# Last V spread from two queues, first group normed and turned directly behind the modulation, new instruction orders

## The chip, the core and the metric
The kernel runs on one core of a Trainium2 chip. The core has five engines with a queue of instructions each: PE (matrix products; PEld is its weight load), DVE, ACT and POOL (elementwise work) and SP, which here only issues DMAs. An engine works its queue strictly in order, and engines wait for each other through semaphores. The metric is the device time of one execution in microseconds, the median of several runs.

## The reference, cut to what matters
Two layers follow each other, all in float32, on x of 32 sequences with 32 tokens of 128 features.

```python
# layer 0: a block with adaptive normalisation, 16 heads of 8 channels
shift, scale, gate, shift2, scale2, gate2 = split(silu(c) @ w_ada + b_ada, 6)
x_mod = ln(x) * (1 + scale) + shift
k, q, v = split(x_mod @ w_qkv, 3)
y = softmax(q @ k.T / 8) @ v                      # per head, 32 keys
x = x + gate * (y @ w_proj + b_proj)
x = x + gate2 * (gelu((ln(x) * (1 + scale2) + shift2) @ w_mlp1 + b_mlp1) @ w_mlp2 + b_mlp2)
# layer 1: graph attention in two directions d over the first 20 tokens
self_feat = concat(x, c or 0) @ W_self.T + b_self
out = self_feat + sum_d(softmax(q_d @ k_d.T / sqrt(8) + mask_d + label_d) @ kv, then Wout_d, + bout_d)
x = x + relu(out)
```

## The kernel before
128 partitions hold four sequences of 32 tokens; eight such groups g = 0 to 7 make the whole input. Layer 0 works up to the attention in five chunks (groups 0; 1; 2-3; 4-5; 6-7), the rest in four pairs of groups. An attention unit is one group (layer 0, units 0 to 7) or one group and direction (layer 1, units 8 to 23: 8 to 11 belong to the first pair of groups, 20 to 23 to the last).

A step is named by its stage and key, as in `('scores', 5)` or `('take', (('v1', 3, 0), 0))`. The list ORDER holds all steps of the kernel in one sequence; ON and TAKE_ON say on which engine a step runs; each engine's queue is ORDER filtered by engine. Nothing else sets the order. `fresh` emits the semaphore waits of a step before it. BANKS gives each step that writes PSUM its bank; the step waits until the earlier user of the bank has been read.

The chain of a unit:
- stats (L1339 to L1344, DVE), rstd (L966, POOL), nmr (L1456, DVE), apply (L1283 ACT, L1462 DVE for chunk 0): normalising. xnT (L1000, PE) turns the result, and its take (L1371, DVE) multiplies with the modulation cmod (L1026 on PE, L1355 on DVE) and writes xm.
- q, k, v (L1056). k is spread by a mask, on POOL (kspread, L773; k1spread, L785) or in four masked copies on ACT (L1223; L1256).
- scores (L1155, PE), in layer 1 badd (L1503, DVE: adds the bias), max (L1517 in layer 0, L1513 in layer 1, DVE), sub (L1528 DVE, L746 DVE or POOL), turn (L1170, L1167, PE), exp (L1310, L1307, ACT), values (L1199, L1190, PE), recip and mult (L1541, L1552, DVE). Units share rings of four buffers.
- V is transposed by DVE out of PSUM (L1385, L1418) into v_raw and then spread into the zeroed Vz by DMA (L884 in layer 0, four DMAs for a chunk; L898 in layer 1, eight for a pair of groups, all issued by SP behind one wait). values waits for all of them.
- mlp1, mlp2, self, selfT, q1, k1, v1 (L1076, L1082, L1090, L1000, L1104, L1106, L1109) and their takes lie between the layers; in layer 1 the steps ya, yb (L755, L766), relu (L1562) and store follow.

In layer 1, three slots of Vz exist, so the spread of the fourth pair waits for the values of the first. The order was found for the whole kernel at once; the work of neighbouring groups and of both layers is interleaved.

Of the kernel before, what the change touches and what calls it, by code (L numbers as in the profile page):

```python
# [62 lines left out]
K1_MASKED = {(0, 1), (1, 1), (2, 1), (3, 1)}  # L63
# [110 lines left out]
 ('k', 3): 1,
 ('q', 3): 3,
 ('v', 3): 2,
 ('xnT', 4): 3,
 ('k', 4): 1,
 ('q', 4): 0,
 ('v', 4): 3,  # L180
 ('scores', 0): 4,
 ('turn', 0): 1,
 ('values', 0): 2,
 ('scores', 1): 4,
 ('turn', 1): 0,
 ('values', 1): 0,
 ('scores', 2): 4,
 ('turn', 2): 1,
 ('values', 2): 2,
 ('scores', 3): 4,  # L190
 ('turn', 3): 2,
 ('scores', 4): 4,
 ('turn', 4): 0,
 ('values', 3): 0,
 ('scores', 5): 4,
 ('turn', 5): 3,
 ('scores', 6): 4,
# [6 lines left out]
 ('yT', 0): 1,
 ('proj', 0): 0,
 ('x1tok', 0): 1,
 ('xn2T', 0): 4,
 ('mlp1', 0, 0): 1,
 ('mlp1', 0, 1): 6,
 ('mlp1', 0, 2): 5,  # L210
# [5 lines left out]
 ('k1', 0, 0): 2,
 ('q1', 0, 0): 0,
 ('k1', 0, 1): 7,
 ('q1', 0, 1): 2,
 ('v1', 0, 0): 6,  # L220
# [8 lines left out]
 ('values', 6): 3,
 ('scores', 11): 4,  # L230
 ('turn', 11): 3,
 ('yT', 1): 2,
 ('proj', 1): 2,
 ('x1tok', 1): 4,
 ('xn2T', 1): 2,
 ('mlp1', 1, 0): 2,
 ('mlp1', 1, 1): 2,
 ('mlp1', 1, 2): 6,
 ('mlp1', 1, 3): 7,
 ('mlp2', 1): 2,  # L240
 ('self', 1): 1,
 ('selfT', 1): 1,
 ('x2tok', 1): 1,
 ('k1', 1, 0): 3,
 ('q1', 1, 0): 3,
 ('k1', 1, 1): 0,
# [14 lines left out]
 ('proj', 2): 3,
 ('x1tok', 2): 4,
 ('xn2T', 2): 4,
 ('mlp1', 2, 0): 7,
 ('mlp1', 2, 1): 5,
# [1344 lines left out]
```

## Time and profile before

| | us |
|---|---|
| median of 3 runs | 92.58 |
| lowest, highest | 91.04, 92.81 |
| the profiled execution | 91.11 |
| its span | 89.4 |

| engine | busy us | share | instructions |
|---|---|---|---|
| PE | 79.5 | 89% | 1768 |
| PEld | 61.0 | 68% | 1768 |
| DVE | 68.4 | 76% | 203 |
| ACT | 51.1 | 57% | 114 |
| POOL | 57.7 | 65% | 82 |

The mean granted TensorE clock was 0.989 of full speed. A line of a timeline gives the start in us, the busy time of the instructions together, the engine, the line of the code, the operation, what it writes and reads, the shapes and how many there are; in brackets the idle time of the engine before them and what ended it. SPq and ACTq are DMA issues of SP and ACT. An fp32 matmul of this kernel shows as two records (or one where a record is missing).

### The profile page before, as it was taken

What the parts mean: (1) busy time and instruction counts of PE and PEld (TensorE: products, weight loads), DVE (VectorE), ACT (ScalarE), POOL (GpSimd) and SP (SyncE); (2) the same over time, 40 slices, a digit from 0 to 9 for tenths busy, and PEclk for the clock granted to TensorE, in tenths of its full rate; (3) what the DMA queues carried; (4) which work ended last, traced back from release to release, by engine and by line L of the source; (5) the groups of instructions that cost most, each with busy time, mean ns of one, the idle gap of its engine ahead of it and who ended that gap; (6) DMA issues with size and microseconds to landing.
All of it is one profiled execution on the core that took longest, in us unless ns stands there. A gap on an engine that the chain in (4) does not pass through costs nothing.

```text
span 89.4 us, 4174 instructions
## 1 busy us (share of the span) xinstructions
PE 79.5 (89%) x1768; PEld 61.0 (68%) x1768; DVE 68.4 (76%) x203; ACT 51.1 (57%) x114; POOL 57.7 (65%) x82
## 2 busy tenths in 40 slices
PE   5997999998999899999999999999989969976810
PEld 5997757655666777878987766778777746645700
DVE  0679899799798865779262699299979997898870
ACT  4823929618456599264697693689526953433310
POOL 7797877999133649784836799703955965085900
PEclk9999999999999999999999999999999999999995
DMA  1878789987412600000001100020002100212041
...
DMA packets 7076, 7.08 MB, mean 79 GB/s; under 512 B 1169, under 2 KB 6193, under 8 KB 7057
## 3 DMA queue, kind: packets, MB, share of 16 engines
...
q8 instruction: 14, 0.23, 1.1%
...
## 4 chain that ended last, share of the span: by engine, by line
PE 72%; DVE 13%; issue 5%; POOL 5%; ACT 1%; DVEq 0%; POOLq 0%; ACTq 0%
PE ps_all L1155 11%; PE ps_all L1076 8%; PE ps_all L1082 8%; PE ps_all L1056 6%; PE ps_all L1000 6%; PE ps_all L1167 5%; PE ps_all L1119 4%; PE ps_all L1170 4%; PE ps_all L1104 4%; PE ps_all L1106 3%; PE ps_all L1199 2%; PE ps_all L1190 2%; DVE E L1503 2%; PE ps_all L1109 2%; PE ps_all L1064 2%
## 5 line engine op out<-in xcount | busy, mean ns | idle before, releaser
L1307 ACT ACTIVATE PT<-ps_all 120x384 f32<-120x384 f32 x16 | 7.5, 489 | 7.3 <-PE ps_all L1167 7.3
L785 POOL TENSOR_TENSOR Kb<-k_raw,head_mask 128x640 f32<-128x640 f32 x4 | 5.0, 1253 | 7.0 <-ACT Kb L1256 4.3
L1239 ACT ACTIVATE hidden<-ps_all,cols 128x256 f32<-128x256 f32 x16 | 7.1, 475 | 3.7 <-PE ps_all L1076 3.7
L1076 PE MATMUL ps_all<-xm,w_rest_sb 128*128 128x256 f32 x32 | 9.1, 387 | 0.0
L966 POOL TENSOR_TENSOR rstd<-var_eps,minus_half 128x2 f32<-128x2 f32 (+1 forms) x9 | 6.0, 665 | 4.7 <-DVE var_eps L1344 4.5
L736 POOL TENSOR_TENSOR xT<-gated,xT 128x256 f32<-128x256 f32 x8 | 5.8, 729 | 4.9 <-DVE gated L1391 3.9
L746 POOL TENSOR_TENSOR E<-E,neg_max 128x320 f32<-128x320 f32 x8 | 6.1, 771 | 3.5 <-DVE neg_max L1513 3.5
L1167 PE MATMUL ps_all<-ident,E 128*120 128x128 f32 x48 | 8.1, 284 | 0.2
L1056 PE MATMUL ps_all<-xm,w_qkv_sb 128*128 128x256 f32 (+1 forms) x30 | 7.5, 360 | 0.5 <-DVE xm L1371 0.5
L1190 PE MATMUL ps_all<-Vz,PT 120*32 120x54 f32 (+1 forms) x384 | 6.2, 208 | 2.0 <-DMA Vz<-v_raw 0.9
L1190 PEld LDWEIGHTS ps_all<-Vz,PT 120*32 120x32 f32 (+1 forms) x384 | 5.2, 109 | 3.8 <-ACT PT L1307 1.3
L1082 PE MATMUL ps_all<-hidden,w_rest_sb 128*128 128x256 f32 x32 | 7.8, 386 | 0.0
L773 POOL TENSOR_TENSOR Kb<-gated,head_mask 128x1024 f32<-128x1024 f32 (+1 forms) x4 | 6.7, 1679 | 1.5 <-ACT gated L1224 1.5
L1155 PE MATMUL ps_all<-Kb,home_b 32*32 32x80 f32 x512 | 7.1, 240 | 0.7 <-issue 0.4
L1513 DVE TENSOR_REDUCE neg_max<-E 128x16 f32<-128x320 f32 x16 | 7.4, 476 | 0.2
L1256 ACT ACTIVATE Kb<-ps_all,bk_masked,head_mask 128x160 f32<-128x160 f32 x16 | 7.1, 490 | 0.7 <-PE ps_all L1106 0.7
L1517 DVE TENSOR_REDUCE neg_max<-ps_all 128x16 f32<-128x512 f32 x8 | 5.5, 691 | 1.8 <-PE ps_all L1155 1.5
L801 POOL MEMSET Vz<- 128x2592 f32 x3 | 6.8, 2257 | 0.0
L1155 PEld LDWEIGHTS ps_all<-Kb,home_b 32*32 32x32 f32 x512 | 3.9, 103 | 4.2 <-issue 2.6
L1082 PEld LDWEIGHTS ps_all<-hidden,w_rest_sb 128*128 128x128 f32 x32 | 5.9, 190 | 1.0
L1310 ACT ACTIVATE PT<-ps_all 128x512 f32<-128x512 f32 x8 | 4.5, 595 | 3.4 <-PE ps_all L1170 3.3
L746 DVE TENSOR_TENSOR E<-E,neg_max 128x320 f32<-128x320 f32 x8 | 6.2, 787 | 0.1
...
## 6 DMA issues: line engine op xcount, KB each, us to landing
...
w_rest_sb<-in_w_rest SPq DMA_DIRECT2D x1, 512.0 KB, 6.0
xT<-in_xT SPq DMA_DIRECT2D x1, 512.0 KB, 5.0
...
```

Source lines behind the costliest of these rows:

```text
L746: return engine.tensor_tensor(e, e, nm_of(n).unsqueeze(2).broadcast_to(list(e.shape)), ALU.add)
L801: return engine.memset(Vz1[:, m, :, :, :, :, :], 0.0)
L1056: return pe.matmul(ps[:, 0:n], w_qkv_sb[:, o:o + P], xm[:, bs, :], start=True, stop=True)
L1076: return pe.matmul(ps[:, 0:n], w_of(W_MLP1 + name[2]), xm[:, bs, :], start=True, stop=True)
L1082: ins = pe.matmul(ps[:, 0:n], w_of(W_MLP2 + j), hidden[:, slot_of(h), j, 0:n], start=(j == js[0]), stop=(j == js[-1]))
L1155: ins = pe.matmul(to[QUAD * b:QUAD * b + QUAD, j, :], qT, Kb, start=True, stop=True)
L1167: ins = pe.transpose(ps[0:KR, c * P:(c + 1) * P], E1[:, r, c * KR:(c + 1) * KR], ident[:, :])
L1190: ins = pe.matmul(ps[QUAD * b:QUAD * b + QUAD, o + c * SIX * CW:o + c * SIX * CW + w], PT[0:n, key % RING, c, b * S:(b + 1) * S], V, start ...
L1239: return act.activation(hidden[:, slot_of(h), j, 0:n], ps[:, 0:n], ACT.Gelu_apprx_tanh, bias=cols[:, R_MLP1 + j:R_MLP1 + j + 1])
L1256: return act.activation(kb1_of(h, d)[:, part, :, :], ps[:, 0:nb * M].rearrange("p (b k) -> p b k", k=M), ACT.Identity, bias=bk_masked[:, d ...
L1307: ins = act.activation(PT[0:KR, key % RING, 0:CH, :], ps[0:KR, 0:CH * P].rearrange("p (j t) -> p j t", t=P), ACT.Exp)
L1513: ins = dve.tensor_reduce(nm_of(key), e_of(key), AX.X, ALU.max, negate=True)
```

## The change
Four things are changed:
- The V spread of a pair of groups in layer 1 is two steps, part 0 (heads 0 to 3 of each six, four DMAs) and part 1 (the other two, four DMAs), each with a semaphore of its own. `('spread', ('v1', 3, 1))` is on ACT's queue, where it stands behind exp 17 and ahead of exp 18; all other parts are on SP. The code of a spread has moved into a function that SP and ACT call.
- The start: `masks` comes before the first statistics; chunk 0 is applied before the statistics of chunk 1, and PE turns it (`xnT`, 0) directly behind the matmuls of `cmod`, 0. Unit 0 is scored before unit 1.
- ORDER is new from one end to the other. Of its steps the four V spreads of layer 1 are replaced by eight; all others are the same.
- BANKS is new, with scores of layer 0 in banks 0 to 3 (before: 4 to 7).

K1_MASKED is the same set in another sequence.

```diff
+V_PARTS = [[(i, i, 0, CH, 0) for i in range(HI)],
+           [(i, (i - HI) * 2 + c, c, c + 1, CH) for i in range(HI, SIX) for c in range(2)]]
...
+ ('spread', ('v1', 3, 1)): 'act',
...
-ORDER = [('zero', 'ones'), ('zero', 'vz0b'), ('consts', 0), ('fetch', 'cols'), ('fetch', 'x0'), ('fetch', 'x1'),
-         ('ident', 0), ('fetch', 'ada0'), ('warm', ('w0', 8)), ('fetch', 'qkv'), ('fetch', 'x2'), ('stats', (0, 0)),
-         ('rstd', (0, 0)), ('stats', (0, 1)), ('silu', 0), ('dense', ('cmod', 0)), ('masks', 0), ('fetch', 'x3'),
-         ('fetch', 'x4'), ('plus1', 0), ('rstd', (0, 1)), ('apply', 0), ('warm', ('w1', 3)), ('nmr', (0, 1)),
-         ('apply', 1), ('take', (('cmod', 0), 0)), ('dense', ('xnT', 1)), ('dense', ('xnT', 0)), ('dense', 'qb'),
...
+ORDER = [('fetch', 'x0'), ('fetch', 'cols'), ('fetch', 'x1'), ('zero', 'ones'), ('warm', ('w0', 8)),
+         ('fetch', 'ada0'), ('fetch', 'qkv'), ('ident', 0), ('zero', 'vz0b'), ('consts', 0), ('silu', 0),
+         ('plus1', 0), ('masks', 0), ('stats', (0, 0)), ('rstd', (0, 0)), ('fetch', 'x2'), ('apply', 0),
+         ('stats', (0, 1)), ('dense', ('cmod', 0)), ('take', (('cmod', 0), 0)), ('dense', ('xnT', 0)),
+         ('rstd', (0, 1)), ('take', (('xnT', 0), 0)), ('fetch', 'x3'), ('fetch', 'x4'), ('warm', ('w1', 3)),
...
             if stage == "spread":
-                return spread_done[key], 16 * (SIX + 2 if key[0] == "v1" else HI)
+                return spread_done[key], 16 * HI
...
+        def spread(engine, name, key):
...
+            m, part = key[1:]
+            for s in fresh(name, *[("take", (("v1", m, d), 0)) for d in range(DIRS)], ("zero", "v1_ones")):
+                engine.wait_ge(*s)
+            for s in fresh(name, *vz1_free(m)):
+                engine.wait_ge(*s)
+            nb, k = bs.stop - bs.start, vslot_of(m)
+            for i, quad, c0, c1, j in V_PARTS[part]:
+                to, of = slice(M * i, M * i + M), slice(QUAD * quad, QUAD * quad + M)
+                engine.dma_start(Vz1[to, k, i, c0:c1, 0:nb, :, :].rearrange("p c b d w -> p c (b d w)"),
+                                 v1_raw[of, j:j + c1 - c0, bs, :, :].rearrange("p c b d w -> p c (b d w)"))\
+                      .then_inc(spread_done[key], 16)
...
-                        for s in fresh("pe", ("spread", ("v1", m))):
+                        for s in fresh("pe", *[("spread", ("v1", m, part)) for part in range(len(V_PARTS))]):
...
+                if stage == "spread":
+                    spread(act, "act", key)
+                    continue
```

The new queues in the places of which the prediction speaks:

```text
DVE, start:  zero ones, masks, stats 0, apply 0, stats 1, take cmod 0, take xnT 0, stats 2, nmr 1, stats 4, nmr 2, take q 0 ...
PE, start:   warm (8), cmod 0, xnT 0, warm (3), vsh, qb, k 0, v 0, q 0, xnT 1, cmod 1, q 1, k 1, xnT 2, v 1, scores 0 ...
ACT, start:  silu, take qb, take k 0 (copy 0), apply 1, take vsh, apply 2, k 0 (2), k 0 (3), take k 1, k 0 (1), apply 3 ...
SP, start:   loads cols, x1, ada0, qkv, x2, x3, x4, ada1, rows, rest0, adj1, xT; spread v 0; adj0; spread v 1; rest1 ...
POOL:        ... kspread 2, zero wx1, zero vz1 0, kspread 3, zero v1_ones, bsum, kspread 4, xb, resid1 0 ...
PE, middle:  ... k1 (1, 0), k1 (1, 1), v1 (0, 0), scores 8, v1 (1, 0), mlp1 (3, 1), scores 9, mlp1 (3, 2), mlp1 (3, 0),
             q1 (1, 1), scores 10, mlp1 (3, 3), self 2, scores 12, turn 8, mlp2 3, scores 14, turn 10, turn 9, selfT 2,
             turn 11, scores 13, values 8, values 9, scores 15 ...
PE, end:     ... turn 17, v1 (3, 1), scores 21, values 15, values 14, scores 20, values 17, turn 19, scores 23, values 16,
             turn 18, scores 22, x2tok 1, turn 20, turn 21, values 18, 19, 21, x2tok 0, values 20, x2tok 2, turn 22,
             turn 23, values 22, 23, x2tok 3
ACT, end:    ... exp 17, spread v1 (3, 1), exp 18, take x2tok 1, exp 19, exp 21, exp 20 ...
DVE, end:    ... max 20, badd 23, recip 9, sub 20, badd 22, mult 9, max 23, max 22, relu 2, recip 10, sub 22 ...
```

## Rows read from the trace of the kernel before

**Rows 1.** Windows by stage: us; busy (and instructions) of PE, PEld, DVE, ACT, POOL; PEclk, DMA share, GB/s
```profile
0.00:30.00 30.00, 27.39 (x582) 20.94 (x583) 23.84 (x79) 16.58 (x34) 21.27 (x36) 1.00 0.63 177
30.00:65.00 35.00, 34.92 (x615) 27.50 (x614) 25.13 (x73) 24.41 (x56) 23.80 (x26) 1.00 0.10 23
65.00:86.60 21.60, 17.20 (x574) 12.58 (x574) 19.40 (x52) 10.08 (x24) 12.66 (x22) 1.00 0.15 39
```
**Rows 2.** Timeline, the start, all engines
```profile
0.80 0.41 ACTq L857 DMA_DIRECT2D x_tok<-in_x_tok  x1
...
2.93 0.29 DVE L1339 BATCH_NORM_STATS2 stats<-x_tok 128x6 f32<-128x128 f32 x1 [1.87 <-DMA x_tok<-in_x_tok]
...
4.69 0.87 PE L1026 MATMUL ps_all<-silu_c,w_ada_sb 128*128 128x32 f32 x4
...
5.60 0.23 DVE L1355 TENSOR_TENSOR cmod<-ps_all,cols 128x64 f32<-128x64 f32 x1 [0.35 <-PE ps_all L1026]
...
6.62 0.49 DVE L1371 TENSOR_TENSOR xm<-ps_all,cmod 128x128 f32<-128x128 f32 x2
...
9.40 1.12 ACT L1223 ACTIVATE Kb<-ps_all,head_mask 128x128 f32<-128x128 f32 x4
```
**Rows 3.** Timeline of DVE, 15 to 28 us: max 2, 3, 5 and 7
```profile
15.29 0.69 DVE L1517 TENSOR_REDUCE neg_max<-ps_all 128x16 f32<-128x512 f32 x1
...
17.88 0.69 DVE L1517 TENSOR_REDUCE neg_max<-ps_all 128x16 f32<-128x512 f32 x1 [0.48 <-PE ps_all L1155]
...
22.82 0.69 DVE L1517 TENSOR_REDUCE neg_max<-ps_all 128x16 f32<-128x512 f32 x1 [0.64 <-PE ps_all L1155]
...
27.77 0.69 DVE L1517 TENSOR_REDUCE neg_max<-ps_all 128x16 f32<-128x512 f32 x1 [0.34 <-PE ps_all L1155]
```
**Rows 4.** Timeline, the V spread of the last pair and its reader
```profile
73.90 0.43 DVE L1418 STREAM_TRANSPOSE v_raw<-ps_all 128x256 f32<-128x256 f32 x1
...
74.36 6.59 SPq L898 DMA_DIRECT2D Vz<-v_raw  x8
...
80.98 0.49 ACT L1307 ACTIVATE PT<-ps_all 120x384 f32<-120x384 f32 x1 [0.47 <-PE ps_all L1167]
...
82.20 0.73 PE L1190 MATMUL ps_all<-Vz,PT 120*32 120x54 f32 x48 [0.86 <-DMA Vz<-v_raw]
```
**Rows 5.** Timeline of DVE and POOL, 65 to 83 us
```profile
65.52 0.49 DVE L1503 TENSOR_TENSOR E<-ps_all,bias_q 128x320 f32<-128x320 f32 x1 [0.41 <-PE ps_all L1167]
...
76.21 0.49 DVE L1503 TENSOR_TENSOR E<-ps_all,bias_q 128x320 f32<-128x320 f32 x1 [0.68 <-PE ps_all L1155]
...
81.27 0.47 DVE L1513 TENSOR_REDUCE neg_max<-E 128x16 f32<-128x320 f32 x1
...
81.89 0.73 POOL L746 TENSOR_TENSOR E<-E,neg_max 128x320 f32<-128x320 f32 x1
...
82.99 0.36 DVE L1541 RECIPROCAL rden<-ps_all 128x32 f32<-128x32 f32 x1 [0.53 <-PE ps_all L1190]
```
**Rows 6.** The chain that ended last, layer 1's PE steps: start, us, what
```profile
42.30 1.73 PE ps_all L1082 x8
...
44.03 0.27 PE ps_all L1109 x2
...
52.97 0.43 PE ps_all L1076 x2
...
53.40 0.55 PE ps_all L1090 x4
...
55.20 0.33 PE ps_all L1167 x3
...
55.96 0.35 PE ps_all L1155 x27
```
**Rows 7.** The second half of the weights: its issue (timeline of SP), its landing (DMA issues)
```profile
10.84 0.59 SPq L857 DMA_DIRECT2D w_rest_sb<-in_w_rest  x1
...
w_rest_sb<-in_w_rest SPq DMA_DIRECT2D x1, 512.0 KB, 6.0
```

More of the change, by code:

```diff
@@ L174 @@
[L174 to L197, printed above, removed]
+ ('v', 1): 7,
+ ('xnT', 2): 4,
+ ('k', 2): 7,
+ ('q', 2): 4,
+ ('v', 2): 6,
@@ L198 @@
+ ('xnT', 3): 5,
+ ('k', 3): 7,
+ ('q', 3): 5,
+ ('v', 3): 5,
+ ('xnT', 4): 7,
+ ('k', 4): 7,
+ ('q', 4): 6,
+ ('v', 4): 5,
+ ('scores', 0): 0,
+ ('turn', 0): 4,
+ ('values', 0): 4,
+ ('scores', 1): 0,
+ ('turn', 1): 6,
+ ('values', 1): 6,
+ ('scores', 2): 0,
+ ('turn', 2): 4,
+ ('values', 2): 4,
+ ('scores', 3): 0,
+ ('turn', 3): 7,
+ ('scores', 4): 0,
+ ('turn', 4): 7,
+ ('values', 3): 6,
+ ('scores', 5): 0,
+ ('turn', 5): 6,
+ ('scores', 6): 0,
  ('turn', 6): 1,
- ('values', 4): 2,
- ('scores', 7): 4,
@@ L201 @@
- ('turn', 7): 2,
- ('bias', 0): 3,
+ ('values', 4): 1,
+ ('scores', 7): 0,
+ ('turn', 7): 4,
+ ('bias', 0): 7,
  ('bias', 1): 3,
[L204 to L210, printed above, removed]
+ ('yT', 0): 7,
+ ('proj', 0): 6,
+ ('x1tok', 0): 5,
+ ('xn2T', 0): 2,
+ ('mlp1', 0, 0): 0,
+ ('mlp1', 0, 1): 5,
+ ('mlp1', 0, 2): 3,
  ('mlp1', 0, 3): 6,
- ('mlp2', 0): 6,
+ ('mlp2', 0): 3,
  ('self', 0): 5,
- ('selfT', 0): 5,
+ ('selfT', 0): 2,
@@ L215 @@
  ('x2tok', 0): 2,
[L216 to L220, printed above, removed]
+ ('k1', 0, 0): 5,
+ ('q1', 0, 0): 4,
+ ('k1', 0, 1): 6,
+ ('q1', 0, 1): 0,
+ ('v1', 0, 0): 2,
  ('v1', 0, 1): 3,
  ('scores', 8): 4,
- ('turn', 8): 1,
- ('values', 5): 6,
+ ('turn', 8): 3,
+ ('values', 5): 1,
  ('scores', 9): 4,
- ('turn', 9): 2,
+ ('turn', 9): 1,
  ('scores', 10): 4,
  ('turn', 10): 3,
[L229 to L246, printed above, removed]
+ ('values', 6): 0,
+ ('scores', 11): 0,
+ ('turn', 11): 0,
+ ('yT', 1): 4,
+ ('proj', 1): 4,
+ ('x1tok', 1): 0,
+ ('xn2T', 1): 4,
+ ('mlp1', 1, 0): 4,
+ ('mlp1', 1, 1): 0,
+ ('mlp1', 1, 2): 3,
+ ('mlp1', 1, 3): 5,
+ ('mlp2', 1): 0,
+ ('self', 1): 5,
@@ L261 @@
[L261 to L265, printed above, removed]
+ ('turn', 15): 1,
+ ('yT', 2): 6,
+ ('proj', 2): 6,
+ ('x1tok', 2): 2,
+ ('xn2T', 2): 5,
+ ('mlp1', 2, 0): 4,
+ ('mlp1', 2, 1): 0,
  ('mlp1', 2, 2): 3,
- ('mlp1', 2, 3): 6,
- ('mlp2', 2): 3,
- ('self', 2): 0,
- ('selfT', 2): 0,
+ ('mlp1', 2, 3): 4,
+ ('mlp2', 2): 4,
+ ('self', 2): 2,
+ ('selfT', 2): 2,
  ('x2tok', 2): 0,
- ('k1', 2, 0): 2,
- ('q1', 2, 0): 2,
- ('k1', 2, 1): 1,
- ('q1', 2, 1): 0,
- ('v1', 2, 0): 5,
@@ L277 @@
- ('v1', 2, 1): 4,
- ('scores', 16): 0,
- ('turn', 16): 1,
- ('values', 9): 2,
- ('scores', 17): 0,
- ('turn', 17): 0,
- ('scores', 18): 0,
- ('turn', 18): 1,
- ('values', 10): 1,
- ('scores', 19): 0,
- ('turn', 19): 2,
- ('yT', 3): 1,
- ('proj', 3): 5,
- ('x1tok', 3): 4,
- ('xn2T', 3): 0,
- ('mlp1', 3, 0): 3,
- ('mlp1', 3, 1): 0,
- ('mlp1', 3, 2): 1,
- ('mlp1', 3, 3): 1,
- ('mlp2', 3): 0,
- ('self', 3): 4,
- ('selfT', 3): 4,
- ('x2tok', 3): 6,
- ('k1', 3, 0): 6,
- ('q1', 3, 0): 4,
- ('k1', 3, 1): 5,
@@ L303 @@
- ('q1', 3, 1): 4,
+ ('k1', 2, 0): 3,
+ ('q1', 2, 0): 0,
+ ('k1', 2, 1): 3,
+ ('q1', 2, 1): 1,
+ ('v1', 2, 0): 1,
+ ('v1', 2, 1): 0,
+ ('scores', 16): 4,
+ ('turn', 16): 4,
+ ('values', 9): 1,
+ ('scores', 17): 4,
+ ('turn', 17): 0,
+ ('scores', 18): 4,
+ ('turn', 18): 2,
+ ('values', 10): 5,
+ ('scores', 19): 4,
+ ('turn', 19): 0,
+ ('yT', 3): 1,
+ ('proj', 3): 6,
+ ('x1tok', 3): 7,
+ ('xn2T', 3): 5,
+ ('mlp1', 3, 0): 0,
+ ('mlp1', 3, 1): 2,
+ ('mlp1', 3, 2): 3,
+ ('mlp1', 3, 3): 3,
+ ('mlp2', 3): 1,
@@ L304 @@
+ ('self', 3): 2,
+ ('selfT', 3): 2,
+ ('x2tok', 3): 4,
+ ('k1', 3, 0): 5,
+ ('q1', 3, 0): 2,
+ ('k1', 3, 1): 2,
+ ('q1', 3, 1): 2,
  ('v1', 3, 0): 6,
- ('v1', 3, 1): 0,
+ ('v1', 3, 1): 1,
  ('scores', 20): 4,
- ('turn', 20): 4,
+ ('turn', 20): 2,
  ('values', 11): 4,
  ('scores', 21): 4,
- ('turn', 21): 3,
+ ('turn', 21): 4,
  ('scores', 22): 4,
- ('turn', 22): 0,
- ('values', 12): 4,
+ ('turn', 22): 6,
+ ('values', 12): 0,
  ('scores', 23): 4,
```

286 lines of the change are left out of this document (137 added, 149 removed).

## The prediction
> **What bounds the kernel now.** I read the stage windows first. They show three regimes [rows 1]. In the first 30 us neither PE (27.39 us busy) nor DVE (23.84) is full: they hand work to each other. From 30 to 65 us PE is busy 34.92 of 35 us and DVE only 25.13: no order of the same work can make that stretch shorter, only a worse one longer. From 65 us to DVE's last instruction at 86.6 it is turned round: DVE is busy 19.40 of 21.60 us, PE 17.20. So what can be won lies in two places, the hand-overs before 30 us and DVE's 2.20 idle us after 65.
>
> Then the timelines of these places. At the start DVE takes the statistics of x's first group from 2.93 on, yet the first xm is made at 6.62 [rows 2]. Of DVE's pauses in the first stage three are waits for scores: 0.48, 0.64 and 0.34 us, 1.46 together [rows 3].
> At the end I read the spread of V. SP issues the eight DMAs of the last pair of groups one after another, 74.36 to 80.95, right behind DVE's transposition at 74.33; values 20 on PE wait for them until 82.20, a pause of 0.86 [rows 4]. ACT's exp of unit 20 was done at 81.47, so 0.7 us of that is DMA alone. DVE then stands 0.53 us before the reciprocal of that pair. The two longest of its other pauses after 65 us are 0.41 for a turn and 0.68 for scores [rows 5].
>
> **The change, part by part.** No compute instruction is added or removed; the DMAs stay 32 for V in layer 1. What changes is place.
>
> *Last V spread from two queues.* Part 1 (four DMAs) goes to ACT, part 0 stays on SP. One DMA issue takes 6.59/8 = 0.82 us; a load issued by ACT took 0.41 [rows 2] and one by SP 0.59 [rows 7], so ACT isn't slower at this, and I price it as SP. Both queues issue 4 × 0.82 = 3.3 us instead of 6.6. From the last issue's end (80.95) to the landing (82.20) is 1.25. If DVE gives V at the same time, it lands at 74.33 + 3.3 + 1.25 = 78.9, well before values 20. Worth: the 0.53 us of DVE, bounds 0 and 0.86. Cost: ACT can do nothing for 3.3 us behind exp 17. Queued behind it are exp 18, the taking of x2tok 1, exp 19, 21 and 20. PE has in this time scores 21, 20, 23, values 15, 14, 17, 16 and turns 19, 18: scores 0.35, turn 0.33 [rows 6], values taken like a turn: 3 × 0.35 + 4 × 0.33 + 2 × 0.33 = 3.0 us, before exp 18 can even start. So the cover is there and I cost it at 0; without it up to 3.3 us would stand in front of exp 18, and PE's values 18 and 19 behind it.
> The Trainium skill (DMA: Bandwidth & Descriptors, Issuing engines are not separate DMA queues) speaks against this part: all queues share the 16 DMA engines, and issuing from several saves only the sequencer's issue time, which it calls usually small. The row agrees on what is saved and not on its size: here issuing is 6.59 us and the rest 1.25. By the rule's "small" the split would be worth nothing and the sum 0.5 less good.
>
> *First group normed and turned behind the modulation.* DVE's order is now masks, stats 0, apply 0, stats 1, taking cmod, xm of group 0; PE turns group 0 directly behind the six modulation matmuls, which end at 5.56. The taking of cmod ends at 5.83, so the first xm begins near 5.85 instead of 6.62: 0.75 us earlier. It isn't gained whole: unit 0 is now the first scored, and it needs all four masked copies of k on ACT. ACT made those from 9.40 to 10.52 [rows 2]; in the new order two applies and k 1 share its queue, and my count of its queue gives the last copy near 10.2. DVE's work ahead of max 2 is the same in both orders, 13.3 us by the durations of its rows. With DVE never idle from 5.6 it reaches max 2 at about 15.1 against 15.29 [rows 3]: worth 0.2.
> *Orders of the rest of layer 0.* The same DVE work lies before max 3, 4 and 5, but their scores stand behind other PE work; xnT 3 and v 3 have moved forward, unit 7 is taken before 6. I take a third of the 1.46 us of score waits, 0.5. Bounds: 0 (a memset of Vz1 now stands ahead of kspread 3 on POOL, so scores 4 may come no earlier) and all 1.46. First stage together: −0.7, from 0 to −1.7.
>
> *The middle.* PE is full, so a shift is worth 0 and a new wait costs in full. One is near. Before, the last of V's matmuls for groups 0 and 1 stood early: from it to the first values of these groups PE had 14.9 us of queued work. In the new order, v1 (0, 0) comes behind k1 (1, 1), and to values 8 lie: 6 scores, 4 mlp1, q1, v1, self, 4 turns, mlp2, selfT = 6 × 0.35 + 4 × 0.43 + 0.43 + 0.27 + 0.55 + 4 × 0.33 + 1.73 + 0.22 = 8.3 us; a turn is three transposes in 0.33, so the two of selfT are 0.22 [rows 6]. V needs, from that matmul: 0.15 to its end, 0.44 to transpose, 6.6 of issuing (both parts still on SP), 1.25 to land: 8.4. The 6.5 us of slack are gone. I take 0.2 us of waiting (0.1 from the sum, 0.1 for DVE finishing another instruction); bounds 0 and 3 (DVE or SP late by a whole queue of work). The next pair's V then lands 6.6 later, at 15.0 from the same matmul; PE comes to values 13 after 16.5: 1.5 to spare.
>
> *The end.* The last four scores have 62.3, 63.3, 64.4, 65.4 us of PE work before them instead of 63.0, 64.0, 64.8, 65.9, summed along PE's queue with such durations: half a microsecond less. The last subtraction is now on DVE (unit 22), and unit 23's on POOL lies in its shadow; before, PE's turn 23 had to wait for max 23 at 81.27 and then POOL, 81.89 to 82.62 [rows 5]. As DVE is full until 84.7, this alone gives DVE little; I take 0.4 of its 0.68 us wait and none of the 0.41. With the V split's 0.53: −0.9, from 0 to −2.2 (all of DVE's idle time).
>
> **Sum**: −0.7 + 0.2 − 0.9 = −1.4. The profiled execution took 91.11 us (span 89.4 and 1.7 around it): it becomes 89.7. The median of the runs is 92.58, 1.47 above the profiled one, which lies at the fast end (91.04 to 92.81). On the median: 91.2.
>
> **Rivals.**
> *A, all of it is recovered.* Both stages get nearly their bounds, −1.3 and −1.6, and the middle has no wait: −2.9, 89.7 on the median. For it: by its own queue counts each score wait of the first stage can go, and three causes of DVE's idle time at the end are touched at once. Against: DVE at 19.40 of 21.60 leaves almost nothing, and every new order brings hand-overs of its own. Chance 0.30 for a gain over 2%.
> *B, nothing net.* The start is eaten by ACT's masked copies, the V split by DVE, which is full anyway; the waits reappear with other names: −0.2 on the sum, 92.4. Here the page's "usually small" would hold. Chance 0.16.
> *C, slower: V of the first two groups is late.* Slack there went from 6.5 us to about 0. Each microsecond by which DVE takes v1 (0, 0) late, or SP starts late, stops PE at values 8, and PE is the bound there. It decides from 3.4 us of stop on if the other gains (−1.6) hold; with 4 us of stop the sum is +2.4, 95.0. For it: two DVE reductions and two additions stand around that take. Against: DVE is busy only 25.13 of 35 us in this stage. Chance 0.09.
> *D, slower: the second half of the weights is late.* Its load was issued at 10.84; now it stands behind the first two V spreads on SP, near 14.4, and what needs it first (qrow) has moved ahead of proj 0, to about 22.2 on PE. With the 6.0 us that it took to land before, it is there at 20.4 [rows 7]: no wait. It decides from 11 us of landing on (3.3 us of stop); with 4 us of stop the sum is +2.6, 95.2. Chance 0.03.
>
> **How the numbers follow.** Forecast 0.42, A 0.30, B 0.16, C and D 0.12. About 2% (1.85 us) is what a measurement of this kernel can tell from no change. Forecast and B fall within it: 0.58; A is faster: 0.30; C and D slower: 0.12. The likeliest time is 91.2; by itself it is good for 90.7 to 92.2. The range leaves out the better end of A and C and D: 89.2 to 93.2.
>
> **What would show it.** In the new profile: first xm near 5.9; max 2 on DVE near 15.1, max 5 before 22.5; PE's wait at values 8 for Vz small; the last V spread 3.3 us long on both queues and no DMA wait of PE after 75 us; an ACT gap of 3.3 us behind exp 17 in which PE keeps working; DVE idle under 1.5 us in its last 21 us. I am wrong if PE stops over 1 us at values 8 or qrow, if ACT's gap holds up exp 18, or if DVE's idle time at the end stays at 2.2 us.

## The result

The changed kernel takes 96.38 us (median of 4 runs, 95.83 to 97.87) beside 92.31 of the kernel before (4 runs on the same chip): ratio 1.051, 95% interval 1.034 to 1.068. It is slower, by 4.1 us. The forecast was 91.2, from 89.2 to 93.2. Ratios in this text leave disturbed runs out, so one can differ a little from the quotient of two medians.

The profiled execution of the changed kernel took 97.87 us, its span is 95.5. The span grew by 6.1 us over the 89.4 of before; this execution is the longest of the four, and the medians differ by 4.1 alone. One other run of it had a mean granted clock of 1.00 and still took 96.64 (span 94.7), so most of the loss doesn't need the lower clock that the profile shows in two places.

Stages of the changed kernel, in the columns of [rows 1]:

```profile
0.00:30.00 30.00, 26.97 (x538) 20.54 (x542) 24.82 (x76) 15.57 (x32) 22.25 (x33) 0.94 0.62 170
30.00:65.00 35.00, 33.52 (x575) 26.72 (x568) 25.62 (x74) 22.19 (x52) 21.19 (x27) 1.00 0.12 27
65.00:92.60 27.60, 21.58 (x664) 16.61 (x662) 18.52 (x52) 13.06 (x31) 14.26 (x23) 0.94 0.10 23
```
In the last stage DVE, which was to be full, is idle for 27.60 − 18.52 = 9.1 us; before it was 2.2. PE is idle there for 6.0 us instead of 4.4. Both kernels run 1,768 MATMUL and 203 DVE instructions; something stands still. Two things are new, one at the start and one at the end.

**The start.** Timeline of DVE and POOL, 5 to 30 us:

```profile
5.89 0.29 DVE L1381 TENSOR_TENSOR xm<-ps_all,cmod 128x128 f32<-128x128 f32 x1
...
7.84 1.99 DVE L1354 TENSOR_SCALAR var_eps<-meanvar 128x2 f32<-128x2 f32 x1
7.91 1.92 DVE L1466 SCALAR_TENSOR_TENSOR nmr<-meanvar,rstd 128x2 f32<-128x2 f32 x1
7.98 1.85 DVE L1385 TENSOR_TENSOR selfT<-ps_all,qb 128x128 f32<-128x128 f32 x1
8.18 1.65 DVE L1381 TENSOR_TENSOR xm<-ps_all,cmod 128x128 f32<-128x128 f32 x1
...
12.67 0.69 DVE L1527 TENSOR_REDUCE neg_max<-ps_all 128x16 f32<-128x512 f32 x1
...
18.22 0.69 DVE L1527 TENSOR_REDUCE neg_max<-ps_all 128x16 f32<-128x512 f32 x1
...
24.83 0.69 DVE L1527 TENSOR_REDUCE neg_max<-ps_all 128x16 f32<-128x512 f32 x1
...
29.76 0.68 DVE L1527 TENSOR_REDUCE neg_max<-ps_all 128x16 f32<-128x512 f32 x1
...
7.79 2.02 POOL L803 MEMSET Vz<- 128x2304 f32 x1
```
The first xm is at 5.89, as forecast. But a `tensor_scalar` on 128x2 elements, 0.17 us elsewhere in the same trace, lasts 1.99 us, and all DVE instructions queued behind it end together with it at 9.83. POOL's memset of Vz ends at 9.81. It began 0.05 us before. (The masks, which the change puts first on DVE, meet the other memset of Vz in the same way: a `tensor_scalar` on 128x4 elements at 1.99 lasts 1.57 us, up to 3.56; that memset ends at 3.50.) The last reduction of layer 0 is at 29.76; before it was at 27.77 [rows 3]: 2.0 us late.

**The end.** Timeline of PE, with the stretches between left out:

```profile
62.70 0.43 PE L1162 MATMUL ps_all<-Kb,home_b 32*32 32x80 f32 x31
64.26 0.22 PE L1162 MATMUL ps_all<-Kb,home_b 32*32 32x80 f32 x1 [1.14 <-issue]
...
68.46 0.40 PE L1162 MATMUL ps_all<-Kb,home_b 32*32 32x80 f32 x25
70.44 0.34 PE L1162 MATMUL ps_all<-Kb,home_b 32*32 32x80 f32 x7 [1.57 <-issue]
...
73.85 0.71 PE L1197 MATMUL ps_all<-Vz,PT 120*32 120x54 f32 x42
75.97 0.27 PE L1197 MATMUL ps_all<-Vz,PT 80*32 80x36 f32 x6 [1.41 <-issue]
...
81.04 0.41 PE L1162 MATMUL ps_all<-Kb,home_b 32*32 32x80 f32 x26
82.40 0.33 PE L1162 MATMUL ps_all<-Kb,home_b 32*32 32x80 f32 x6 [0.94 <-issue]
```
Four times PE stops in the middle of one operation, a run of 32 or 48 like matmuls whose inputs are all there, for 0.94 to 1.57 us, and the profile names no engine and no DMA as the releaser, only "issue". The same four are in the chain that ended last. They sum to 5.1 us. Counted along the whole timeline, there are 126 or 127 matmuls from one stop to the next, each with a weight load; in TensorE's own sequence of records the stops are 256 apart to the record. The page's DMA part has a queue of kind instruction, q8, with 13 packets and 0.21 MB: 16 KB each, about one for every 256 of the 3,536 records (1,768 matmuls and as many weight loads). The places at which PE stops are the ends of these blocks. The kernel before has block ends too, and a stop of 0.38 us at one near 78.7. A fifth block end lies at 86.72, in a wait of 0.93 us that the profile puts on ACT, whose exponential ended 0.13 us before; which of the two PE waited for is open.

The clock is a third thing. From 11.5 to 14.9 us and from 76.3 to 79.7 the granted clock is half, 1.2 GHz instead of 2.4, each time shortly after PE had stood idle (up to 9.95, up to 75.97); in the profile of before it is full up to PE's last matmul. The same two matmuls at either level, timeline of PE:

```profile
65.83 0.43 PE L1113 MATMUL ps_all<-selfT,w_rest_sb 128*128 128x160 f32 x2
...
76.74 0.74 PE L1113 MATMUL ps_all<-selfT,w_rest_sb 128*128 128x160 f32 x2
```
The six steps from 76.17 to 79.89 take 3.7 us where rows at full clock add up to 2.0: an estimate of 1.7 us for the second stretch. PE's busy time grew from 79.5 to 82.1 us in all.

The account: 2.0 us at the start, 5.1 − 0.4 at the block ends and 1.7 for the clock make 8.4, more than the 6.1 that the span grew. Against them stand two waits of before that are gone, the 0.86 for V [rows 4] and one of 0.81, in the timeline of PE before:

```profile
73.08 0.73 PE L1190 MATMUL ps_all<-Vz,PT 120*32 120x54 f32 x48 [0.81 <-DVE v_raw L1418]
```
Such terms can't simply be added, since a stop of PE may hide behind another engine. How much of the forecast's gains was left isn't shown by this sum.

The Trainium skill (Runtime: NRT & Kernel Launch, Instruction fetch mechanics) has instructions fetched in 16 KiB blocks of 256 and calls the cost of a crossing "mostly hidden". The blocks agree with the trace. The cost doesn't: 0.9 to 1.6 us at each of four.

### The profile page after: what moved, and what is told of

Same layout as the page of the kernel before. It is cut to its first block, busy times and chain, and to the rows that moved or that the text cites. A ratio compares the mean times of both kernels' runs of the same rounds, so it can differ in the third digit from the quotient of the medians.

```text
span 95.5 us, 4187 instructions
## 1 busy us (share of the span) xinstructions
PE 82.1 (86%) x1768; PEld 63.9 (67%) x1768; DVE 69.8 (73%) x203; ACT 50.8 (53%) x114; POOL 57.7 (60%) x82
## 4 chain that ended last, share of the span: by engine, by line
PE 60%; DVE 17%; issue 10%; POOL 7%; ACT 4%; DVEq 0%; POOLq 0%
PE ps_all L1162 12%; PE ps_all L1174 6%; PE ps_all L1089 6%; PE ps_all L1083 5%; PE ps_all L1007 5%; PE ps_all L1063 5%; PE ps_all L1177 4%; PE ps_all L1111 4%; PE ps_all L1197 3%; DVE nmr L1466 3%; PE ps_all L1116 2%; POOL Vz L808 2%; PE ps_all L1113 2%; ACT xn_tok L1238 2%; DVE head_mask L1457 2%
## 5 line engine op out<-in xcount | busy, mean ns | idle before, releaser
L1162 PE MATMUL ps_all<-Kb,home_b 32*32 32x80 f32 x512 | 7.6, 240 | 3.9 <-issue 3.7
L743 POOL TENSOR_TENSOR xT<-gated,xT 128x256 f32<-128x256 f32 x8 | 6.4, 802 | 6.1 <-issue 4.5
L1063 PE MATMUL ps_all<-xm,w_qkv_sb 128*128 128x256 f32 (+1 forms) x30 | 8.2, 401 | 0.4 <-DVE v_raw L1395 0.4
L1197 PE MATMUL ps_all<-Vz,PT 120*32 120x54 f32 (+1 forms) x384 | 6.7, 208 | 1.8 <-issue 1.4
L1174 PEld LDWEIGHTS ps_all<-ident,E 128*120 128x120 f32 x48 | 5.7, 144 | 2.2 <-ACT PT L1317 1.2
L1428 DVE STREAM_TRANSPOSE v_raw<-ps_all 128x256 f32<-128x256 f32 x8 | 4.0, 498 | 4.0 <-PE ps_all L1116 3.9
L1513 DVE TENSOR_TENSOR E<-ps_all,bias_q 128x320 f32<-128x320 f32 x8 | 3.9, 489 | 3.5 <-PE ps_all L1162 3.5
L1063 PEld LDWEIGHTS ps_all<-xm,w_qkv_sb 128*128 128x128 f32 x30 | 5.4, 218 | 1.5 <-DVE v_raw L1395 0.9
```

What stands on the lines that cost most here:

```text
L1063: return pe.matmul(ps[:, 0:n], w_qkv_sb[:, o:o + P], xm[:, bs, :], start=True, stop=True)
L1162: ins = pe.matmul(to[QUAD * b:QUAD * b + QUAD, j, :], qT, Kb, start=True, stop=True)
L1174: ins = pe.transpose(ps[0:KR, c * P:(c + 1) * P], E1[:, r, c * KR:(c + 1) * KR], ident[:, :])
L1197: ins = pe.matmul(ps[QUAD * b:QUAD * b + QUAD, o + c * SIX * CW:o + c * SIX * CW + w], PT[0:n, key % RING, c, b * S:(b + 1) * S], V, start ...
```

## The experiments

**1. The start: memset or something else.** First the two memsets of Vz cut into eight pieces each, so that DVE could get in between.

```
- return engine.memset(Vz0[:, 0:2, :, :, :], 0.0)
+ for b0 in range(0, B, B // 8):
+     ins = engine.memset(Vz0[:, 0:2, b0:b0 + B // 8, :, :], 0.0)
+ return ins        # the same for Vz0[:, 2:4]
```


> The changed kernel, with each of the two memsets of Vz0 on POOL cut into eight (same bytes, same place). Theory P (a POOL memset holds back DVE's tensor_scalar from SBUF to SBUF, and all that is queued behind it): var_eps at 7.84, which took 1.99 us and ended with the memset, takes under 0.4; the first scores start 1.5 to 2 us earlier; the clock doesn't fall between 11 and 14 us, as PE no longer stands idle from 7.7 to 9.9; total 94.0 (2 to 2.5 less than 96.4). The five stops of PE after 60 us stay (theory I). Rival (the DVE instructions are slow for another reason, such as a late load): no change, 96.4.

Measured: 97.94 us (95.28 to 102.19), too scattered to tell a gain from none; 94.0 was forecast. Its timeline of POOL and DVE:

```profile
8.06 2.29 POOL L804 MEMSET Vz<- 128x288 f32 x8
...
8.11 2.27 DVE L1358 TENSOR_SCALAR var_eps<-meanvar 128x2 f32<-128x2 f32 x1
```
DVE is held for all eight pieces. Cutting the memset frees nothing; this neither shows nor refutes that it is the holder. The next edit takes away the other side, the form of DVE's instruction, with the same result ((v + eps) max v):

```
- dve.tensor_scalar(var_eps, meanvar[..., 1], LN_EPS, None, ALU.add)
+ dve.scalar_tensor_tensor(out=var_eps, in0=meanvar[..., 1], scalar=LN_EPS,
+                          in1=meanvar[..., 1], op0=ALU.add, op1=ALU.max)
```


> The changed kernel, where var_eps (variance plus epsilon, from SBUF to SBUF on DVE) is made by a scalar_tensor_tensor ((v + eps) max v) instead of a tensor_scalar: same values, same place in the order. Cutting POOL's memset into pieces had not freed DVE. Theory P2 (a tensor_scalar from SBUF to SBUF waits for as long as POOL has memsets in a row, whatever their size; another form of instruction doesn't): the instruction near 7.9 takes 0.2 instead of 2.0 us, xm of chunks 1 and 2 come 2 us earlier, PE doesn't stand idle from 8 to 10 and its clock doesn't fall near 11 to 14. The five stops of PE at the block ends stay somewhere: total 93 to 95. Rival P3 (any DVE instruction would wait there): 96.4.

Measured: the profiled execution took 94.82 (span 93.1), the others up to 99.8; with that scatter the total tells nothing, and the timeline has to. Its timeline of DVE and POOL:

```profile
7.99 0.16 DVE L1354 SCALAR_TENSOR_TENSOR var_eps<-meanvar 128x2 f32<-128x2 f32 x1
...
10.56 0.97 DVE L1467 SCALAR_TENSOR_TENSOR nmr<-meanvar,rstd 128x2 f32<-128x2 f32 x1
11.46 0.68 DVE L1528 TENSOR_REDUCE neg_max<-ps_all 128x16 f32<-128x512 f32 x1
...
10.48 1.04 POOL L780 TENSOR_TENSOR Kb<-gated,head_mask 128x512 f32<-128x512 f32 x1
```
At the same time, under the same memset, the instruction now lasts 0.16 us, and the first reduction comes at 11.46 instead of 12.67. So the memset holds this form of `tensor_scalar` (SBUF to SBUF) and what is queued behind it, and not the form with two inputs. This is shown. The Trainium skill (SBUF — State Buffer, SBUF: two separate sides) states it: the port pair that VectorE shares with GpSimd is locked for a whole instruction by the one that comes first, where the VectorE instruction runs in a mode of two ports, or has two inputs in SBUF and GpSimd's reads SBUF. The trace agrees; that eight memsets in a row keep it too is what these runs add. The second case is there as well: the two-input `nmr` at 10.56, 0.15 us elsewhere in the trace, lasts 0.97 and ends at 11.53, with POOL's k spread, which reads SBUF and ends at 11.52. So the form with two inputs is free of memsets, not of everything on POOL. Of PE's issue waits this kernel has 5.3 us, so the second cause is untouched.

The same edit in the kernel before, where the hold is only 0.5 us (`var_eps` at 6.54, under a memset up to 7.03):

> The kernel before with var_eps by scalar_tensor_tensor. There one such instruction overlaps a memset (6.54, 0.52 us, up to the memset's end at 7.03). Theory P2: 0.3 us earlier xm, total 0 to 0.5 less: 91.8 to 92.3. No theory expects more.

Measured: 92.86 (92.01 to 95.41, 4 runs); no gain can be told. The instruction lasts 0.16 us there, but this execution stood 1.39 us at the block end near 23 us, where the profile of before shows 0.28.

**2. The end: is it the place in the instruction stream?** If a block end costs when it falls into dense work, moving all block ends must change the time, in both kernels. 32 matmuls of 16 columns on an unused bank are 64 MATMUL and 64 weight loads: 128 records.

```
+ if key == ('xnT', 1):
+     for i in range(32):
+         q = slice(QUAD * (i % UB), QUAD * (i % UB) + QUAD)
+         pe.matmul(ps_all[q, 7, 0:16], ones[:, 0:QUAD], ones[:, 0:16], start=True, stop=True)
  ins = dense_product(key)
```


> The changed kernel with 32 tiny matmuls (128 instruction records of PE) put in front of xnT 1, where PE waits anyway; nothing else changes. Theory I (PE's five stops of 1.0 to 1.8 us at records 2241, 2497, 2753, 3009 and 3265, always 256 apart, are waits for the next block of 256 instructions): the stops stay at these counts of records but meet other work, 128 records earlier; sizes change, and the total moves by 1 to 5 us, more likely down, to 93.5. Rival W (the stops belong to the work there, for instance to a semaphore or to DMA traffic of the V spreads): stops stay with the same scores and values, total 96.4 to 97.0.

Measured: 92.16 us, ratio to before 0.999 (0.991 to 1.006). 0.74 us of extra work makes the kernel 4.2 us faster. Its waits of PE:

```profile
PE ps_all L1166 <- issue: 1.7, 1, 1.7
PE ps_all L1210 <- issue: 0.2, 1, 0.2
```
against these of the changed kernel without it:

```profile
PE ps_all L1162 <- issue: 3.7, 3, 1.6
PE ps_all L1197 <- issue: 1.4, 1, 1.4
```
The control has no less PE time in the same place (1.06 us), but 16 records: four matmuls of 128 columns.

> Control for the kernel with 128 more records: the changed kernel with four matmuls of 128 columns at the same place, about the same 0.8 us of PE work, but 16 records instead of 128. Theory I: the block ends move by only 16 records, so most of the stops stay: 95 to 97. Rival K (the extra work kept PE busy and so its clock or its queue in a better state, the number of records is nothing): 92.2, as with the 32 tiny matmuls.

Measured: 96.40, ratio 1.041 (1.035 to 1.047), and 5.3 us of issue waits. It is the number of records and not PE's activity. The packets show it too: from 62 us to the last stop they start 0.6 to 1.5 us behind the block ends with 128 extra records, and up to 3.9 behind them in the control. The mirror image, 128 records in the kernel before, ahead of its ('q', 0):

> The kernel before with 32 tiny matmuls (128 records of PE) behind qb, where PE waits 0.6 us for xm. Theory I: the old order too depends on where the blocks of 256 end; stops of PE of 0.5 to 1.8 us appear at multiples of 256 after record 193, and the total is 1 to 4 us longer, 94.5. Rival W: 92.3 to 92.7.

Measured: 95.28 us, with 3.9 us of issue waits instead of 0.7; the longest, 1.37 and 2.15, lie before 24 us. Three of the four runs took 95.2 to 95.8, the fourth 92.58, so the 3.1 us of the median aren't firm. Nor are stops fixed by the place alone. With the block ends of before untouched, the one near 23 us cost 0.28 us in the profile of before and 1.39, 1.55 and 0.82 in the profiles of three kernels that differ from it elsewhere (the other form of `var_eps`, and the two with a split of V below). All issue waits of the four sum to 0.7, 1.9, 2.2 and 1.0 us; the changed kernel has 5.1.

Two other shifts of the changed kernel:

> The changed kernel with 16 extra 128x32 matmuls of 16 columns (64 instructions' worth of records with their weight loads, about 0.4 to 0.7 us of TensorE time) ahead of the projection of xnT of group 1. Theory I (TensorE stops at every 256th record of its own stream, and pays only where that place falls in work that is dense at the time): all later block ends move 64 records earlier in the work, so other work is hit; the stops are still 256 records apart. Total between the 92.2 of 128 extra records and the 96.4 of none, say 93 to 96.5. Theory K (the extra work itself, by its activity, is what helped): 16 matmuls give half of what 32 gave, 94.3. Theory that the changed kernel is slower by its own order: 96.4.

> As the run with 16 extra matmuls, with 48 of them (192 records). Theory I: the block ends stand 192 records earlier in the work, which is also 64 later; the stops 256 apart again, total 92 to 96 and not in line with the amount of extra work. Theory K: more extra work helps more or as much, 92 or less. Its own cost is about 1.2 to 2.2 us of TensorE time in a stretch where TensorE has idle time.

Measured: 92.44 (ratio 1.022, 1.004 to 1.039) and 94.50 (1.020, 0.979 to 1.062). All three shifts have a lower median than the unshifted kernel, and not in line with the amount of extra work. Only the interval of the shift by 128 (0.991 to 1.006) is clear of that of the unshifted kernel (1.034 to 1.068); the other two overlap it.

**3. What a block end costs by itself.** 384 such matmuls (1,536 records) in one stream, at a place where they wait for nobody.

> The changed kernel with 384 extra 128x32 matmuls of 16 columns (1536 records) in one stream ahead of the product for cmod, so that TensorE has six block ends in a stream that waits for no other engine. Theory I (the fetch of the next 256 instructions takes 2.2 to 2.8 us from its packet to TensorE's resumption, and is behind where 256 records are run off quickly): each block of 256 takes at least about 3.5 us, with a stop of 1 to 2 us at the same place of each block, and the total is 18 to 25 us above 96.4. Rival: the stops need another cause (a queue, a semaphore of another engine, the DMA traffic of the weights); then the stream runs through at the rate of the tiny matmuls, 64 records in 0.40 to 0.74 us, 1.6 to 3.0 us for 256, with no stop at fixed distance.

Measured: 122.19 us, one run, 25.8 above 96.4 where 18 to 25 were forecast. Timeline of PE, the stream (the extra matmuls are L1131):

```profile
4.83 1.92 PE L1131 MATMUL ps_all<-ones 128*32 128x16 f32 x207
12.18 1.90 PE L1131 MATMUL ps_all<-ones 128*32 128x16 f32 x128 [5.43 <-issue]
16.73 1.91 PE L1131 MATMUL ps_all<-ones 128*32 128x16 f32 x128 [2.65 <-issue]
20.46 1.90 PE L1131 MATMUL ps_all<-ones 128*32 128x16 f32 x128 [1.82 <-issue]
23.91 1.90 PE L1131 MATMUL ps_all<-ones 128*32 128x16 f32 x128 [1.55 <-issue]
27.37 0.84 PE L1131 MATMUL ps_all<-ones 128*32 128x16 f32 x49 [1.55 <-issue]
```
Each piece is 128 matmuls and 128 weight loads, 256 records, then a stop; the first piece runs over one block end, at 5.50, without any. So the instructions of two blocks were there. From 16.73 on a block takes 3.5 to 3.7 us, of which it works 1.9, at half the clock. (At full clock, in the next run, such a block works 1.25 us and stops 2.20: 3.45 again.) In the DMA records the packet starts 1.1 us behind the block end and PE resumes 2.3 to 2.6 us behind the packet's start; that makes the 3.5. The first two stops, 5.43 and 2.65, fall into the loading of the weights: with the 16 DMA engines up to nine tenths busy there, the packet starts 4.2 and 2.0 us behind the block end. A block whose work takes over 3.5 us should not stop.

The first stop of the changed kernel, at 63.1, is of this kind: its block holds 3.1 us of work and its packet starts 1.5 us behind the block end. By that alone the next four blocks, 3.4 to 5.5 us of work each, would hardly stop. Their packets start late: 3.6, 2.8, 4.2 and 1.9 us behind the block end, where those of before, from 52 us on, start 0.7 to 1.1 behind it. From packet to resumption it is 2.2 to 2.8 us in both, as in the stream. Two runs ask what starts the fetch. In them some matmuls of the stream are 128-column ones:

```
+ if i in slow:   pe.matmul(ps_all[:, 7, 0:128], ones[:, :], ones[:, 0:128], start=True, stop=True)
+ else:           pe.matmul(ps_all[q, 7, 0:16], ones[:, 0:QUAD], ones[:, 0:16], start=True, stop=True)
```


> The changed kernel with a stream of extra matmuls ahead of the product for cmod, 16-column ones as in m1_stream, but in each block of 256 records 16 of the 128 matmuls are 128x128 ones of 128 columns (0.22 to 0.25 us each, so 3.5 to 4 us of work): right behind the block end (blocks 3 and 5), 56 matmuls behind it (block 4), 96 behind it (block 6). Theory T1 (the fetch of the next block starts only when TensorE has passed some 32 records of this one; then the place of slow work counts): with the slow matmuls first, the packet comes 3.5 us or more behind the block end and TensorE stops again for 1.5 to 2 us at its end; with them at 56 or 96, the packet comes 1.1 us behind the block end and there is no stop. Theory T2 (the fetch starts at the block end itself): the packet comes 1.1 us behind it in every block, and since each block now takes over 5 us there is no stop in any of them.

Each matmul of the source is two MATMUL instructions in the trace, so the 128-column matmuls came 158, 126, 158 and 30 records behind block ends, and blocks without any lay between. Measured: 144.22 us, one run; the blocks with slow matmuls end with no stop, those without with 1.0 to 2.5 us (4.5 in the loading of the weights, where the packet started 3.8 us behind the block end); the other packets 0.9 to 1.5 us behind the block ends, and up to 0.2 ahead of two that slow matmuls led up to. No slow group began at a block end, so the theories weren't told apart. The next run puts them there:

> As m2_slow_places, whose blocks of tiny matmuls alone each ended in a stop and whose blocks with slow matmuls 126 or 158 records in did not; its packets came 0.9 to 1.5 us behind the block ends. Here the 16 slow matmuls (64 records, some 4 to 6 us) stand 2 records behind a block end in two blocks, and 34 records behind it in a third, each with a block of tiny ones before it. Theory T1 (the fetch starts when about 32 records of the block have been executed; in the changed kernel the packets fit this, 1.0 to 1.4 us behind the 32nd): packets 2.5 to 4 us behind the block ends of the first two, about 1.2 behind that of the third. Theory T2 (TensorE's sequencer runs ahead of execution and asks at the block end, unless a wait for another engine holds it): about 1.1 us in all three.

Measured: 132.72 us, one run.

```profile
19.40 0.18 PE L1134 MATMUL ps_all<-ones 128*32 128x16 f32 x1 [1.82 <-issue]
19.51 6.25 PE L1131 MATMUL ps_all<-ones 128*128 128x128 f32 x32
25.69 2.05 PE L1134 MATMUL ps_all<-ones 128*32 128x16 f32 x223
29.70 0.18 PE L1134 MATMUL ps_all<-ones 128*32 128x16 f32 x1 [1.95 <-issue]
29.80 3.84 PE L1131 MATMUL ps_all<-ones 128*128 128x128 f32 x32
```
In this timeline of PE a block end is at 19.40, 6.25 us of slow matmuls follow, and the packet starts at 20.52, 1.12 us behind the block end; at the other two that slow matmuls follow 1.1 as well. T1 falls: executing the first records doesn't hold up the fetch. The block that holds them, 19.40 to 26.49, has no stop at its end; the tiny one behind it, 26.49 to 27.74, has one. Behind the loading of the weights the tiny blocks take 3.2 to 3.8 us here with their stops.

So streams that wait for nobody fetch 1.1 us behind the block end, and the dense stage of the changed kernel up to 4.2 us behind it. What differs is that there PE's instructions wait for other engines; a sequencer held at such a wait would ask late. That was not tried, and it stays open.

**4. The V split by itself.** It was a term of the sum. First taken out of the changed kernel (part 1 of the last pair back on SP):

```
-  ('spread', ('v1', 3, 1)): 'act',
```


> The changed kernel with part 1 of the last V spread back on SP, behind part 0. Theory I and P: the loss doesn't come from the split; 96.4 to 97.2, with a later landing of the last V. Rival S (ACT's 3.3 us of issuing holds up exp 18 and all behind it): 3 us gained, 93.4.

Measured: 97.24, ratio 1.054 (1.048 to 1.061) to before, beside 1.051 (1.034 to 1.068) with the split. The loss isn't the split. In its profile PE has no wait for the last V even with all eight issues on SP, so no run shows that the split is worth anything in the new order. Then the split alone, put into the kernel before:

```
+  ('spread', ('v1', 3, 1)): 'act',
- ... ('exp', 17), ...  ('spread', ('v1', 3)), ...
+ ... ('exp', 17), ...  ('spread', ('v1', 3, 0)), ('spread', ('v1', 3, 1)), ...
```


> The kernel before with the V spread of layer 1 in two parts, and the second part of the last pair issued by ACT; its orders, banks and everything else as before. This is one part of the change alone. TensorE's instruction stream keeps its length, so its block ends stand where they stood. Forecast for this part: the 0.53 us of DVE ahead of the last reciprocal, so 0.5 less than before (0 to 0.9). Rival (the loss of the change comes from the split): 1 us or more above before, up to the 3.3 us that ACT issues.

Measured: 96.30, ratio 1.050 (1.033 to 1.067). Timeline of SP, ACT and PE:

```profile
78.87 3.27 SPq L879 DMA_DIRECT2D Vz<-v_raw  x4
...
84.11 3.60 ACTq L879 DMA_DIRECT2D Vz<-v_raw  x4
...
88.95 1.09 PE L1193 MATMUL ps_all<-Vz,PT 120*32 120x54 f32 x48 [3.10 <-DMA Vz<-v_raw]
```
SP issues its part at 78.87; ACT comes to its own only at 84.11, behind the taking of x2tok 1, and values 20 waits 3.10 us. (This execution also stopped 1.55 us at the block end near 23 us, so not all of its loss is the split's.) With the part directly behind exp 17, as in the change:

```
- ('exp', 17), ...  ('spread', ('v1', 3, 0)), ('spread', ('v1', 3, 1)), ...
+ ('exp', 17), ('spread', ('v1', 3, 1)), ...  ('spread', ('v1', 3, 0)), ...
```


> As b4_before_split, but the second part stands directly behind the exponential of unit 17 on ACT, as in the changed kernel, and not behind the taking of x2tok 1, where ACT came to it 5 us later than SP to its part. Forecast: 0.5 less than before (0 to 0.9) and no wait of TensorE for V above 0.9 us. Rival: the exponential of unit 18, now 3.3 us later on ACT, holds up values 18 and 19, and the kernel is 1 to 3 us slower than before.

Measured: 94.75, ratio 1.031 (1.014 to 1.047). Timeline of ACT and PE:

```profile
75.92 3.60 ACTq L879 DMA_DIRECT2D Vz<-v_raw  x4
79.56 0.38 ACT L1268 ACTIVATE home_b<-ps_all 128x256 f32<-128x256 f32 x1 [3.22 <-issue]
79.84 0.49 ACT L1313 ACTIVATE PT<-ps_all 120x384 f32<-120x384 f32 x1
80.00 1.19 PE L1193 MATMUL ps_all<-Vz,PT 120*32 120x54 f32 x48 [2.66 <-ACT home_b L1268]
```
V is no longer late, but ACT's four issues stand in front of the taking of x2tok 0 and exp 18, and PE's values wait 2.66 us for them. The rival of this run holds. The gap of ACT was free only where PE has 3.3 us of other work, and the old order hasn't got it.

**5. Both causes taken away.** `var_eps` by the other form, with 128, 160 and 64 extra records:

> Both edits: var_eps by scalar_tensor_tensor, and 128 more records of PE ahead of xnT 1. Theory I with P2: the gains add up, 92.2 less 1.5 to 2.5 from the start: 90.2, faster than both kernels. Rival (the start's 2 us are hidden later, as the first stage waits for loads and POOL anyway): 92.

> The changed kernel with var_eps by scalar_tensor_tensor (not held back by GpSimd's memset) and 40 extra matmuls (160 records). Both causes removed as far as this shift does it: with the forecast's own -1.4 on the kernel before, 91.0 if no stop of over 1 us is left; 93 to 94 if, as with 128 records, one stop of 1.5 us stays at the last block end but one. Theory I says only that the stops are 256 records apart.

> The changed kernel with var_eps by scalar_tensor_tensor and 16 extra matmuls (64 records). With 64 records alone the profiled run had no stop over 1 us between 27 and 82 us and was at 92.2. If the 1.3 to 1.8 us that DVE wins at the start by the other instruction reach the end, 91.0; if TensorE's stops eat them (they move with every change of the times), 92 to 94.

Measured: 93.58 (ratio 1.002, 0.996 to 1.008); 94.26 (91.44 to 97.44, no ratio); and 90.36 (ratio 0.994, 0.990 to 0.999). The last is the only kernel of this study that is faster than the one before, by 0.6%, with five of seven runs between 90.19 and 90.46 (the median of all ten runs of before on that chip is 92.17). Two things were forecast otherwise: the gains of the form and of 128 records were to add up to 90.2, and 160 records with no long stop to 91.0. Timeline of PE and DVE with 64 records:

```profile
17.93 0.68 PE L1210 MATMUL ps_all<-Vz,PT 128*32 128x36 f32 x32 [1.06 <-DMA Vz<-v_raw]
...
23.62 0.49 PE L1181 MATMUL ps_all<-ident,E 128*128 128x128 f32 x3 [1.71 <-issue]
...
19.23 0.69 DVE L1532 TENSOR_REDUCE neg_max<-ps_all 128x16 f32<-128x512 f32 x1 [1.28 <-PE ps_all L1166]
...
25.45 0.69 DVE L1532 TENSOR_REDUCE neg_max<-ps_all 128x16 f32<-128x512 f32 x1 [0.44 <-PE ps_all L1166]
```
Its reductions had come at 11.46, 13.61 and 15.87, so ahead of the changed kernel by up to 2.4 us. Two waits take that back. The first is new: with the hold gone, PE comes to the first values of layer 0 before their V has been spread and waits 1.06 us for the DMA; the lead is 1.2 us at the fourth reduction (19.23 against 20.38). The second is the block end; behind it the sixth reduction is at 25.45 and the changed kernel's was at 24.83. With the form and 128 records the same wait for V is 2.14 us, and the fourth reduction comes at 21.10. So with the memset out of the way, the V spread of layer 0 is what the start waits for next; no run moved it.

## Why the prediction was wrong, step by step

**First group normed and turned directly** (0.2 us gained). The first xm came at 5.89, as said. Max 2 came at 18.22 instead of 15.1. Max 5 came at 24.83, and not before 22.5. The step that failed is the 13.3 us of DVE work "by the durations of its rows" with DVE "never idle": an instruction that POOL's memset holds for 1.99 us had 0.5 in the trace of before. The prediction had read that the orders of POOL and DVE change and did not ask which POOL instruction would now stand beside which of DVE. Max 2 is 3.1 us later than forecast. The run with the other form has it at 15.80, so 2.4 of the 3.1 hang on the memset: 1.2 are there at the first reduction already (12.67 against 11.46), and the half clock from 11.5 to 14.9 lies behind it. The other 0.7 are a miss of the same kind: in that run `nmr`, 0.15 us in the trace of before, is held to 0.97 beside POOL's k spread, as shown in experiment 1.

**Orders of the rest of layer 0** (0.5). Of the score waits of 1.46 us [rows 3] only 0.16 is left, but DVE itself comes 2 us later, so this doesn't show that the order removed them. In the run with the other form alone they are 0.7 us, PE waits 0.8 us for the V of layer 0, which no term priced, and the last reduction is at 28.01: without the hold too the first stage is 0.2 us later than before (27.77), where 0.7 earlier was forecast.

**V split** (0.5). The wait of 0.86 us is gone, but it is gone without the split too (experiment 4), so the term's worth isn't shown. Places as said: both queues issue at 80.48, SP for 3.31 us and ACT for 3.90, and PE has no DMA wait behind 75 us. Timeline of the changed kernel, ACT and PE:

```profile
80.48 3.90 ACTq L883 DMA_DIRECT2D Vz<-v_raw  x4
85.06 0.49 ACT L1317 ACTIVATE PT<-ps_all 120x384 f32<-120x384 f32 x1 [5.03 <-PE ps_all L1174]
...
86.72 0.87 PE L1174 MATMUL ps_all<-ident,E 128*120 128x128 f32 x6 [0.93 <-ACT PT L1317]
```
ACT's gap is 5.03 us, its exponential of 85.06 waits for PE and not for the queue: the cover was there, in this order. That it is the order's and not the split's is what the two kernels before with a split show. The forecast priced the cover right and its absence too: "without it up to 3.3 us", measured 2.66.

**The middle** (0.2 lost) and rival C. No wait of PE for Vz shows in the profile of the changed kernel; C did not happen. Nor did D: no wait for the second half of the weights.

**The end** (0.9). DVE was to be idle for less than 1.5 us in its last 21; it was 9.1 in the last 27.6. The step that failed isn't a term of the sum but something that no term stands for: the sum took PE's durations from rows in which it hardly stopped for instructions, and at full clock, and took it that the same matmuls in another order need the same time. In their place the runs showed 5.1 us of stops at block ends and an estimated 1.7 us of half clock behind the third. Other work now stands at the block ends, and the packets start late; why they do stays open. The trace of before had the sign, a wait of PE on "issue" of 0.38 us near 78.7 in the middle of 32 like matmuls, and it was passed over as small.

Rivals C and D were each a new wait that outweighs the gains, and what happened is of that kind, but neither of them; the range ended at 93.2 with 12 in 100 for all that is slower. With shifts of 64 to 192 records the same change measures 92.2 to 94.5. With the other form as well its best is a gain of 0.6% on the kernel before, of 1.5% forecast, and with one stop of 1.7 us left in it. That is the best of three shifts, beside a kernel before whose own shifts were tried only once; it isn't the worth of the order. How much of the 1.4 us would be there without any stop is not shown.
